# Three small steps of a router, moved from VectorE to GpSimd, in a decoder layer

## The reference, cut to what matters

```python
logits = x @ Wg + bg                         # 8 experts
probs = softmax(logits)
topk_vals, topk_idx = top_k(probs, 2)
mask = one_hot(topk_idx, 8).sum(axis=-2)     # 1 for each of the two chosen experts
probs = probs * mask / (probs * mask).sum(-1)
h = gelu(x @ W1[e] + b1[e]);  y = h @ W2[e] + b2[e]    # for each expert e
out = sum over e of probs[e] * y[e]
```

## Time and profile before

| | |
|---|---|
| median of 3 executions | 1449.48 us (1447.78 to 1449.57) |
| profiled execution | 1462.83 us, its span 1461.0 us, granted TensorE clock 0.989 |
| loop over tiles | about 62 to 1141 us of the span |
| experts and output | from there to the end |
| VectorE busy | 1064.0 us (73%), 3951 instructions |
| GpSimd busy | 927.0 us (63%), 1287 instructions |
| ScalarE busy | 1167.4 us (80%), 4154 instructions |

### The profile page before, as it was taken

How to read it: one execution, slowest core, us unless ns; L and a number is a source line. 1 busy time by engine, 2 the same in 40 slices (tenths; PEclk the granted TensorE clock), 3 DMA queues, 4 the chain that set the end, 5 groups by cost and what they waited for, 6 DMA issues and landing times.

```text
span 1461.0 us, 37538 instructions
## 1 busy us (share of the span) xinstructions
PE 1382.7 (95%) x10832; PEld 1301.2 (89%) x10832; DVE 1064.0 (73%) x3951; ACT 1167.4 (80%) x4154; POOL 927.0 (63%) x1287
## 2 busy tenths in 40 slices
PE   5799999999999999999999999999999989999884
PEld 4699999999999999999999999999998879999881
DVE  4567888788888887888887888888766656556663
ACT  3589888888888888888888888888887657777663
POOL 4455676676667677666666676666654455656664
PEclk9999999999999999999999999999999999999997
DMA  3111111211111211111112111117201457888855
GB/s 96 56 38 38 46 47 52 58 45 48 45 46 49 62 46 47 45 45 47 47 47 60 46 47 45 45 48 128 53 11 61 137 170 242 255 248 278 268 180 180
DMA packets 130964, 129.67 MB, mean 89 GB/s; under 512 B 11811, under 2 KB 115113, under 8 KB 130761
## 3 DMA queue, kind: packets, MB, share of 16 engines
q1 hardware_dynamic: 112216, 105.79, 25.3%
q0 software_dynamic: 8832, 16.94, 3.4%
q10 hardware_dynamic: 9712, 4.53, 1.1%
HBM read 70.83 MB, written 57.30 MB: 88 GB/s over the span
## 4 chain that ended last, share of the span: by engine, by line
PE 53%; DVE 23%; ACT 11%; issue 8%; POOL 2%; DMA 1%; another core or an unknown queue 1%; DVEq 0%; ACTq 0%; SPq 0%; POOLq 0%
ACT probs L761 10%; PE ps_s L1593 9%; DVE neg_max L1108 7%; PE ps_o L1609 6%; PE ps_pT L1619 5%; DVE pT_lo L1119 4%; PE ps_t L1851 4%; PE ps_o L1851 3%; DVE mask L1177 3%; PE ps_t L1633 2%; PE ps_t L1630 2%; PE ps_t L1631 2%; PE ps_u L1648 2%; PE ps_u L1649 2%; PE ps_u L1650 2%
## 5 line engine op out<-in xcount | busy, mean ns | idle before, releaser
L761 ACT ACTIVATE probs<-ps_s,neg_max 128x128 f32<-128x128 f32 x1024 | 362.6, 366 | 139.6 <-DVE neg_max L1108 133.0
L540 POOL TENSOR_TENSOR probs_n<-probs,inv_sum 128x512 f32<-128x512 f32 x256 | 267.3, 1044 | 183.4 <-DVE inv_sum L1114 181.0
L1593 PE MATMUL ps_s<-kvT,u_sb 128*128 128x128 f32 x2048 | 275.3, 277 | 0.4 <-issue 0.4
L1609 PE MATMUL ps_o<-value_w,tT 128*128 128x128 f32 x2048 | 260.0, 275 | 1.2 <-ACT tT L779 1.1
L1593 PEld LDWEIGHTS ps_s<-kvT,u_sb 128*128 128x128 f32 x2048 | 254.1, 191 | 6.8 <-issue 0.4
L1609 PEld LDWEIGHTS ps_o<-value_w,tT 128*128 128x128 f32 x2048 | 243.9, 192 | 1.8 <-ACT tT L779 1.5
L1119 DVE TENSOR_TENSOR pT_lo<-ps_pT,pT_hi 128x512 fp32r<-128x512 f32 x256 | 175.3, 685 | 80.6 <-ACT pT_hi L770 79.1
L761 ACT ACTIVATION_READ_ACCUMULATOR probs<-ps_s,neg_max 128x1 f32 x1024 | 207.5, 203 | 0.0
L655 POOL DMA_INDIRECT y_rows<-wvT,f_x x142 | 142.3, 1002 | 101.4 <-issue 53.4
L553 POOL DMA_INDIRECT x_rows<-routed,pos_i x128 | 136.8, 1068 | 105.9 <-issue 98.1
L1108 DVE TENSOR_REDUCE neg_max<-ps_s 128x4 f32<-128x512 f32 x256 | 175.9, 687 | 18.3 <-PE ps_s L1593 6.0
(11 more groups left out here) (288 smaller groups left out, 3599.1 us busy)
## 6 DMA issues: line engine op xcount, KB each, us to landing
u_sb<-in_expert_w SPq DMA_DIRECT2D x71, 578.0 KB
x_rows<-pad_row SPq DMA_DIRECT2D x66, 520.0 KB, 4.9
f_x<-x_rows SPq DMA_DIRECT2D x71, 130.0 KB
tT<-y_rows SPq DMA_DIRECT2D x16, 512.0 KB
x_raw<-in_x SPq DMA_DIRECT2D x64, 64.0 KB, 1.8
c_raw<-in_ctx_in SPq DMA_DIRECT2D x64, 64.0 KB, 2.0
out<-value_w ACTq DMA_DIRECT2D x16, 256.0 KB
y_rows<-wvT,f_x POOLq DMA_INDIRECT x142
```

Source lines behind the costliest of these rows:

```text
L540: nc.gpsimd.tensor_tensor(probs_n[:, sl], probs[:, sl], inv_sum[:, sl, :].rearrange("p (u o) -> p u o", o=1).to_broadcast([P, UP, P]), ALU ...
L761: last = nc.scalar.activation(probs[:, sl, j], ps_s[sl][:, j * P:(j + 1) * P], ACT.Exp, bias=neg_max[:, sl, j:j + 1], accum_out=sums[:, sl ...
L1593: last = nc.tensor.matmul(ps_s[sl][:, j * P:(j + 1) * P], u_sb[:, c // 2, BT * p + b, h:h + 2].rearrange("p h s -> p (h s)"), kvT[:, c, 2 ...
L1609: last = nc.tensor.matmul(ps_o[:, 0:D], tT[:, (p + 1) % 2, h], value_w[:, h], start=(h == 0), stop=(h == H - 1))
```

## The change

`gate_mask`, `seen_add` and the two copies of `route_rows` leave VectorE and become GpSimd operations with the same operands. VectorE keeps the weight (L1190). In GpSimd's loop `seen_add(t - 4)` stands in unit 0 behind the roots of the norms, ahead of the second `scale`; the copies (`routed_rows(t - 4)`) in unit 2 behind the root for queries and keys, ahead of the fourth `scale`; `gate_mask(t - 3)` in unit 3 behind the indirect DMA. `gate_picked` on VectorE gets a wait on `mask_done`, since its buffer is now read by another engine. Behind the loop the same calls stand between `result_out(i)`. VectorE's calls are gone.

```diff
+            def gate_mask(j):
+                q = j % 2
+                pool.wait_ge(picked_done, j + 1)
+                pool.wait_ge(rank_ps, count(j - 1))
+                nc.gpsimd.tensor_tensor(mask[:, q], picked[:, q, 0], picked[:, q, 1], ALU.add).then_inc(mask_done, 1)
+
+            def seen_add(j):
+                q = j % 2
+                pool.wait_ge(mask_done, j + 1)
+                pool.wait_ge(seen_done, j + 1)
+                pool.wait_ge(rank_ps, count(j))
+                nc.gpsimd.tensor_tensor(seen[:, 1 - q], seen[:, q], mask[:, q], ALU.add).then_inc(seen_done, 1)
+
+            def routed_rows(j):
+                q = j % 2
+                pool.wait_ge(x_routed[q], count((j - q) * 16))
+                pool.wait_ge(x2_done, j + 1)
+                settle(pool)
+                nc.gpsimd.tensor_copy(routed[:, q, :, 0:D],
+                                      rows[:, one(j % ROWS_RING), :].to_broadcast([P, 2, D])).then_inc(rows_kept, 1)
+                nc.gpsimd.tensor_copy(routed[:, q, :, D + 1:D + 2].bitcast(I32).rearrange("p s o -> p o s"),
+                                      rids[:, one(j), :]).then_inc(rids_kept, 1)
...
+                    if k == 0 and on(t, -4):
+                        seen_add(t - 4)
                     if k == 2 and on(t, 5):
                         qk_rstds(t + 5)
+                    if k == 2 and on(t, -4):
+                        routed_rows(t - 4)
                     if k == 3 and on(t, -4):
                         route(t - 4, p, 0)
+                    if k == 3 and on(t, -3):
+                        gate_mask(t - 3)
...
+            seen_add(NT - 4)
+            gate_mask(NT - 3)
+            routed_rows(NT - 4)
             for sl in range(2):
                 route(NT - 4, NT % 2, sl)
             for i in range(NF + 4):
...
                 if i == 0:
                     z2_rstds(NT - 1)
+                    gate_mask(NT - 2)
+                    seen_add(NT - 3)
                 if i == 1:
+                    routed_rows(NT - 3)
...
+                if i == 3:
+                    gate_mask(NT - 1)
+                    seen_add(NT - 2)
                 if i == 5:
+                    seen_add(NT - 1)
                     for j in range(NT - 2, NT):
+                        routed_rows(j)
                         for sl in range(2):
                             route(j, j % 2, sl)
...
                 def gate_picked():
                     dve.wait_ge(atf_done, t - 2)
+                    dve.wait_ge(mask_done, count(t - 4))
...
-                def gate_mask():
-                    dve.wait_ge(picked_done, t - 2)
-                    nc.vector.tensor_tensor(mask[:, p3], picked[:, p3, 0], picked[:, p3, 1], ALU.add).then_inc(mask_done, 1)
...
-                def seen_add():
-
-                    dve.wait_ge(mask_done, t - 3)
-                    dve.wait_ge(rank_ps, t - 4)
-                    nc.vector.tensor_tensor(seen[:, 1 - p], seen[:, p], mask[:, p], ALU.add).then_inc(seen_done, 1)
...
-                    dve.wait_ge(x2_done, t - 3)
-                    settle(dve)
-                    nc.vector.tensor_copy(routed[:, p, :, 0:D],
-                                          rows[:, one((t - 4) % ROWS_RING), :].to_broadcast([P, 2, D])).then_inc(rows_kept, 1)
-                    nc.vector.tensor_copy(routed[:, p, :, D + 1:D + 2].bitcast(I32).rearrange("p s o -> p o s"),
-                                          rids[:, one(t - 4), :]).then_inc(rids_kept, 1)
```

More of the change, by code:

```diff
@@ L1237, in period @@
                     gate_picked()
-                    gate_mask()
                 if part == "inverse":
                     gate_inverse()
-                if part == "seen":
-                    seen_add()
                 if part == "place":
@@ L1273, in period @@
                     z1_sum(t + 4)
-                if on(t, -4):
-                    seen_add()
                 if on(t, 4):
@@ L1340, in period @@
                     place_sum()
-                if on(t, -3):
-                    gate_mask()
                 if on(t, -4):
@@ L1486, in _ @@
             period(NT, 0, "x2")
-            period(NT, 0, "seen")
             period(NT, 0, "place")
@@ L1498, in _ @@
             period(NT + 1, 1, "x2")
-            period(NT + 1, 1, "seen")
             period(NT + 1, 1, "place")
@@ L1506, in _ @@
             ffn(5)
-            period(NT + 2, 2, "seen")
             period(NT + 2, 2, "place")
             ffn(6)
-            period(NT + 3, 3, "seen")
             period(NT + 3, 3, "place")
```

## The result

The changed kernel takes 1429.49 us (median of 4 executions, 1429.06 to 1430.31), the kernel before 1449.22 us beside it (4 executions, 1447.78 to 1449.57). The ratio is 0.9866, with a 95% interval from 0.9849 to 0.9883: 19.7 us less. The forecast was 1427.5 us. After's profiled execution took 1429.28 us, with a span of 1427.5 us.

What follows compares the result with a forecast made beforehand. TensorE was taken as the bound, held up by VectorE's `seen`: 55 periods x (17.03 - 16.60) = 23.6 us, less 1.5 for list periods, leaves 22 us off the median 1449.48: 1427.5 us, range 1421 to 1446.

Steps and rivals of the forecast that it cites:

- What bounds the kernel: TensorE nearly full, but held up each period before `ps_pT` by VectorE's `seen` waiting 0.76 us for `probs_n`.
- The floor: TensorE's own work per period: 16.60 us against 17.03 us, giving 23.6 us over 55 periods.
- The list periods: Five middle periods carry VectorE's list arithmetic, about 1 us each, 0.7 of it covered; 1.5 us taken off the gain.
- `seen` on GpSimd: Add ahead of the second `probs_n`: 0.2 us, 0.28 with the step on, against 0.61 us of cover; nothing paid.
- The copies: Two copies into `routed` ahead of GpSimd's fourth `probs_n`: 0.5 plus 0.16 us against 0.62 us of cover; nothing taken off.
- turning point at 1.05 us: GpSimd's port time for the copies, 0.62 + 0.43 us, from which the change would make the kernel slower.
- slower: Rival: copies at scaling rate, 1.58 us, VectorE waits for all, period 17.56 us, 1478 us; chance 0.14.
- half used up: Rival: copies hold the port 0.85 us or third `probs_n` slips; TensorE stalls 0.2 us a period, 1438.5 us; chance 0.22.
- `mask`: Add in unit 3, 0.96 us on VectorE: no gain counted, since the cast into `pos_i` takes over the wait.
- The tail and the last periods: About 4 us of GpSimd work behind the loop, put at 0 ± 1 us; last four periods' 1 us or more left out.

Runs made afterwards that it cites:

- both runs made for it: Changed kernel with six additional 256-column copies on GpSimd ahead of the copies into routed, 1435.77 us; changed kernel with two 128-column one-tensor scalings there instead, 1430.65 us.
- the second profile of before: The kernel before, profiled once more with nothing changed: 1448.33 us in the profiled execution.

## Why the prediction was right, step by step

**What bounds the kernel.** Right. The run with `seen` moved ahead shows that without its wait for the first `probs_n` an ordinary period falls to what TensorE's own work takes. Of the 0.76 us of the wait 0.34 came back. The wait is not alone on its path, though. The chain of before in order of time leads through unit 3 as well:

```profile
603.68 0.93 DVE mask L1177
...
604.63 0.68 DVE pT_lo L1119
```

Then follow `yT`, `neg_max` and the exponentials, up to `inv_sum` and `seen`. With `seen` moved ahead, `mask` still takes its 0.96 us and the period is 16.63 us, so in an ordinary period this wait alone holds nothing up. With `mask` alone moved, and the cast waiting in its place, the stretch became 0.08 us shorter and the period 0.04 us. No run takes away the wait of unit 3 and leaves that of `seen`, so it isn't shown that only the end of `seen`'s wait frees TensorE.

**The floor.** 16.60 us was taken from one short period of seven (16.60 to 16.65); after's ordinary period is 16.63 us. For the fifty ordinary periods the sum had 50 x (16.96 - 16.60) = 18.0 us, and 16.5 us came.

**The list periods** are the term that was mis-sized most. The sum leaves 0.3 us above the floor for each, 1.5 us in all; after has 3.2 us above 16.63, 0.65 each. The step that failed is "of which 0.7 is covered once `seen` and the copies are gone". `seen` and the copies stand behind the list steps, behind `neg_max` and behind `lT_lo`; they cover nothing for `lT_lo` (the rest of the latents that rounding leaves, which TensorE's matmuls into `ps_u` need), and that is what comes late. The chain of waits of after, period 38, shows it:

```profile
712.80 0.39 DVE yT L1040 x2
713.19 0.09 DVE list_end L1103
...
713.71 0.18 DVE list_row L1106
...
714.52 0.29 DVE lT_lo L1073
714.81 0.04 issue
714.86 0.39 PE ps_u L1662
```

TensorE's `ps_u` waits for `lT_lo`, and the list steps stand ahead of it. Its timeline has the idle time:

```profile
714.86 0.39 PE L1662 MATMUL ps_u<-lT_hi,score_hi 128*128 128x256 f32 x1 [0.23 <-DVE lT_lo L1073]
```

I had not asked which deadline follows them. Moved into idle time they cost nothing, which shows the cause.

**`seen` on GpSimd.** Right: 0.20 us, as priced. `rows` takes 1.22 us beside `probs_n`, much as in the earlier trace rows, and the period isn't lengthened.

**The copies.** The price is right, 0.39 + 0.24 = 0.63 us (taken: 0.66), partly by luck: 0.11 us too much for the large copy and 0.08 too little for the small one. The verdict "no cost" is right too, but the reckoning behind it isn't. I had VectorE wait for all of the copying, with 0.62 us of cover and a turning point at 1.05 us. In fact the change's copies cost VectorE 0.26 us, in one instruction (`cosb`, 0.55 us instead of 0.29), which uses up the idle time before the fourth `inv_sum`, and six copies more cost it another 0.22 us. What has to carry the copies is GpSimd's own slack: the idle 0.87 us ahead of the fourth `probs_n` and 1.82 us behind it. That is read from the timelines; no run went beyond this slack, so the new turning point isn't shown. The chance of "slower" rested on VectorE waiting for all of it, and both runs made for it refute it.

Two figures of the rivals don't come out as stated. By the slope the copy is 0.65 us, not 0.69, so "half used up" would hold VectorE for 0.81 us. And twice 800 ns is 1.6 us; 1.42 comes out only with a start of some 0.18 us counted once, which the prediction doesn't say. The forecast hangs on neither.

The Trainium skill (SBUF — State Buffer, section Who interferes with whom) says that a VectorE instruction with two SBUF inputs contends with a GpSimd instruction that reads SBUF, and that the later of the two is blocked for the whole of the other. With `probs_n`, which reads two tensors, the trace agrees: 0.91 against 0.16 us for `seen`. With copies and one-tensor scalings, which read SBUF too, it mostly doesn't: 0.28 us for `kv_prod` inside 2.45 us of copies, though `picked` grows from 0.16 to 0.36 us there. The measurement decides.

**`mask`.** That the cast takes over the wait is right: 0.85 us instead of 0.16. That nothing is gained is off by 2 us: the pair cost 0.08 us more than the cast alone, and half of that reached TensorE in each period.

**The tail and the last periods.** The end of the loop gave 1.6 us, which I had named and left out. The rest takes 307.4 us in after and 306.0 in the second profile of before, so perhaps 1.4 us were lost there. Over the nine kernels with a readable profile and no additional copies or scalings, the rest ranges from 306.0 to 308.0 us, so this is at the limit of what single profiles tell.

**The sum by parts:** 16.5 + 2.3 + 1.6 = 20.4 us in the loop, less up to 1.4 us behind it, against 19.7 us between the medians. The forecast had 22: 1.5 too much in the floor, 1.9 too much in the list periods, and 1.6 left out on the other side. That the total is off by only 2 us is in part such an offset.

## What to carry to other kernels

When a tiny instruction takes as long as a large one of the neighbouring engine, ask what started just before it; the cure may be to start it 0.3 us earlier, and moving work away is only one way to get there. Before a small step is put into idle time, look at what the other engine runs in that window: the same cast took 0.17, 0.85 or 1.31 us by its place, and the worst place, for it and two steps with it, cost 37 us. And for each step in the code that is not in every period, follow what stands behind it until the next engine that waits, since its cover is only what lies between those two.

## What the hardware showed that I had not expected

- GpSimd's plain copy of 256 fp32 columns takes 0.39 us in after and 0.51 to 0.54 us in the run with two copies more. The estimate from its other instructions was between 0.2 and 1.4.
- VectorE's instructions don't wait for the whole of everything that GpSimd reads. Beside the product `probs_n`, a cast of two columns takes 0.85 us; beside copies, 0.17 us. Why one input and two should differ so, no run here tells.
- In the run with the placing steps together the cast began 0.23 us before the third `probs_n` (590.91 against 591.14) and still ended with it. An indirect DMA ran on GpSimd when the cast began. VectorE's `lT_lo` of 128 columns, with two inputs from SBUF, begins beside an indirect DMA in 51 periods of after and takes its usual 0.28 us in 49 of them. Whether the cast waited for the DMA, or for the product from its start on, was not tried.
